# Decoder layer on one core: transposing q and k by DMA, and a new written-out order over more stages

## The chip, the core and the metric

The program runs on one core of a Trainium2 chip. The core has TensorE (matrix products, into PSUM), VectorE (DVE), ScalarE (ACT), GpSimd (POOL) and SyncE (SP, which here only issues DMAs). The engines run their own instruction streams and meet through semaphores. The metric is the device time of one execution in microseconds (us), lower is better.

## The reference

A pre-norm decoder layer on x of shape (32, 112, 256), batch by batch: attention, a cross block on ctx_1024 (32, 375, 256) that has a gelu in place of a softmax, and a quantised feed-forward block of 256, 1024, 256. Cut to its core:

```python
q = jnp.einsum('bim,mhd->bhid', x, wq)      # 8 heads of 128; k and v likewise
q = _rope(_rmsnorm(q)); k = _rope(_rmsnorm(k))
s = jnp.einsum('bhid,bhjd->bhij', q * mult, k * mult)   # minus 1e30 on later keys
p = jax.nn.softmax(s, axis=-1)
o = jnp.einsum('bhij,bhjd->bhid', p, v)
return jnp.einsum('bhid,hdm->bim', o, wo)
...
x = x + _L0_attn_ref(_layernorm(x, axis=-1), wq, wk, wv, wo)
x = x + _L0_xattn_ref(_layernorm(x, axis=-1), ctx_1024, ctx_1024)
x = x + _L0_ffn_ref(_layernorm(x, axis=-1), w1, b1, w2, b2)
```

## The kernel before, in words

The 32 batches are independent; one batch has 112 rows, which lie on 112 partitions. Every engine has one function `body(i)` that holds its work of round i for several batches at once: a = i is projected, b = i-1 goes through attention, c = i-2 through the cross block and the feed-forward's first layer, d = i-3 through its last. The order inside a body is written by hand for each engine; semaphores count finished steps. Rounds up to 3 and from 28 on are written out, those between run in a loop of four bodies (`iterations`).

Precision is had by splitting operands. A weight or activation is held as a rounded high half and the rest as a low half, and three products (high-high, high-low, low-high) are summed in PSUM. `project` (L846) forms q, k and v with 12 products of 512 columns each. q and k are squared on ScalarE (L697), summed on VectorE (L468), and the root is taken on GpSimd (L349, L351). The rotary step is a product with the cosines (L476), one with the sines (L485) and their sum (`turn`, L492), all on VectorE. `normalise_q` (L743, ScalarE, eight instructions) and `normalise_k` (L497, VectorE, one) scale by the root into `qkn` in fp32. TensorE transposes qkn by heads into PSUM (`transpose_qk`, L854, 16 matmul records a batch), ScalarE rounds the result to fp16 (`split_qkT`, L670) and VectorE forms the low half (L538). `scores` (L833, 24 products of 112 columns) follows, then exp, the causal mask on GpSimd (L362), `weigh_values` (L874), the division, `transpose_o` (L881), the split of oT (L545) and `project_out` (also L833, 24 products of 256 columns). The cross block is L911 (`ctx_hidden`) and L920 (`ctx_out`); the feed-forward is L937 (`hidden_units`) and L945 (`out_units`), with `x3b` = x3 + b2 on GpSimd (L355).

SyncE issues per round the store of a finished batch, `ctx_in` (L267) and `ctxT` (L270) of 375 KB each once the cross block has freed their buffers, and x (L264) of 112 KB.

## Time and profile before

| | us |
|---|---|
| median of 3 runs (lowest to highest) | 731.2 (730.33 to 732.17) |
| the profiled execution, device time | 730.79 |
| its span, first to last instruction | 729.1 |
| TensorE busy | 697.2 |
| VectorE busy | 642.4 |
| ScalarE busy | 486.9 |
| GpSimd busy | 248.3 |

The span is what the views of the trace divide. Busy time of an engine is the time in which it ran an instruction; an engine that is nearly always busy and carries the chain of work that ended last sets the time. Consecutive instructions of an engine overlap a little, so the distance from start to start is shorter than the duration. Matmul ends are modelled, so for TensorE too starts are the better measure.

### The profile page before, as it was taken

Reading aid. Unit: us, or ns where it says so; the run is one execution under the profiler, and the core shown is the slowest. Engines: PE = TensorE matmul, PEld = TensorE weight load, DVE = VectorE, ACT = ScalarE, POOL = GpSimd, SP = SyncE. Lnnn points to the kernel's source line nnn. Section 1 sums busy time; section 2 is a strip of 40 time slices with the busy share of each in tenths; the row PEclk is TensorE's granted clock in tenths of the full one; section 3 lists DMA queues with packets and bytes.
Section 4 is the critical chain, followed back from the end, with each engine's and each line's share of the span. In section 5 each row is a group of like instructions: output and inputs, shape, how many; then the busy total and the mean of one; then the engine's idle time right before and its main releaser. Section 6 shows DMA issues by size and latency. Waiting matters only on the chain.

```text
span 729.1 us, 15114 instructions
## 1 busy us (share of the span) xinstructions
PE 697.2 (96%) x5504; PEld 609.9 (84%) x5504; DVE 642.4 (88%) x1232; ACT 486.9 (67%) x1226; POOL 248.3 (34%) x393
## 2 busy tenths in 40 slices
PE   5599999999999999999999999999999999999974
PEld 4488888888888888888888989889888888888863
DVE  6989999999999999999999999999999999998942
ACT  5667766677766677776667767666777766677742
POOL 1344333433332343333234243333334333433310
PEclk9899999999999999999999999999999999999996
DMA  8501110111111011111111111101111110111100
GB/s 268 204 8 49 49 48 24 54 57 49 55 48 42 26 55 55 48 52 51 32 35 55 55 48 48 52 22 47 55 53 50 48 47 24 54 50 43 49 7 13
DMA packets 23946, 38.86 MB, mean 53 GB/s; under 512 B 2048, under 2 KB 18896, under 8 KB 23664
## 3 DMA queue, kind: packets, MB, share of 16 engines
q1 hardware_dynamic: 23920, 38.51, 17.5%
q8 instruction: 16, 0.26, 0.2%
q14 instruction: 10, 0.08, 0.0%
HBM read 34.84 MB, written 3.67 MB: 53 GB/s over the span
## 4 chain that ended last, share of the span: by engine, by line
PE 89%; DVE 3%; ACT 3%; issue 2%; DMA 2%; SPq 0%; POOL 0%; POOLq 0%; DVEq 0%; ACTq 0%
PE psum L846 34%; PE psum L833 17%; PE psum L874 7%; PE psum L854 6%; PE psum L911 6%; PE psum L920 6%; PE psum L945 4%; PE psum L937 3%; PE psum L881 3%; PE psum L902 2%; DMA w_raw<-in_wv 1%; DMA w_raw<-in_w 1%; ACT qkn L743 1%; PE psum L927 1%; DVE turn_c L492 0%
## 5 line engine op out<-in xcount | busy, mean ns | idle before, releaser
L846 PE MATMUL psum<-wqkv_hi,xnT_hi 128*112 128x512 f32 x384 | 165.1, 430 | 4.8 <-DVE wqkv_lo L433 2.8
L846 PE MATMUL psum<-wqkv_lo,xnT_hi 128*112 128x512 f32 x384 | 152.3, 397 | 0.0
L846 PE MATMUL psum<-wqkv_hi,xnT_lo 128*112 128x512 f32 x384 | 131.4, 396 | 0.0
L697 ACT ACTIVATE sq<-psum 112x1024 f32<-112x1024 f32 x64 | 65.5, 1023 | 79.7 <-PE psum L846 79.7
L344 POOL TENSOR_TENSOR rstd<-ve,nhalf 112x1 f32<-112x1 f32 x96 | 55.4, 578 | 156.0 <-DVE ve L407 151.0
L351 POOL TENSOR_TENSOR rms<-ms,nhalf 112x8 f32<-112x8 f32 x64 | 106.3, 1662 | 5.0
L733 ACT ACTIVATE w_raw<-psum,rden 112x128 f32<-112x128 f32 x256 | 69.5, 384 | 45.7 <-DVE rden L519 45.7
L846 PEld LDWEIGHTS psum<-wqkv_hi,xnT_lo 128*112 128x112 f32 x384 | 67.5, 176 | 22.1
L846 PEld LDWEIGHTS psum<-wqkv_hi,xnT_hi 128*112 128x112 f32 x384 | 68.1, 177 | 21.4 <-issue 3.1
L476 DVE TENSOR_TENSOR turn_c<-psum,cos_t 112x1024 f32<-112x1024 f32 x64 | 78.1, 1220 | 6.2 <-ACT sq L697 5.6
L468 DVE TENSOR_REDUCE ss<-sq 112x4 f32<-112x512 f32 (+1 forms) x95 | 81.9, 862 | 0.0
L846 PEld LDWEIGHTS psum<-wqkv_lo,xnT_hi 128*112 128x112 f32 x384 | 68.4, 178 | 16.1
L743 ACT ACTIVATE qkn<-turn_c,rms 112x128 f32<-112x128 f32 x256 | 81.4, 400 | 0.1
L833 PE MATMUL psum<-wo_hi,oT_hi 128*112 128x256 f32 x256 | 78.3, 306 | 0.8 <-DVE oT_lo L545 0.8
L492 DVE TENSOR_TENSOR turn_c<-turn_c,turn_s 112x1024 f32<-112x1024 f32 x64 | 77.9, 1217 | 0.1
L485 DVE TENSOR_TENSOR turn_s<-psum,sin_t 112x1024 f32<-112x1024 f32 x64 | 77.5, 1210 | 0.0
L833 PE MATMUL psum<-wo_hi,oT_lo 128*112 128x256 f32 x256 | 71.6, 280 | 0.0
L833 PE MATMUL psum<-wo_lo,oT_hi 128*112 128x256 f32 x256 | 71.6, 280 | 0.0
L538 DVE TENSOR_TENSOR qkT_lo<-psum,qkT_hi 128x896 f16<-128x896 f32 x64 | 69.4, 1085 | 0.2
L757 ACT ACTIVATE f_int<-psum,b_col 128x112 int16<-128x112 f32 x256 | 65.8, 375 | 1.8 <-PE psum L937 1.8
L874 PEld LDWEIGHTS psum<-v_sb,w_raw 112*112 112x112 f32 x512 | 60.8, 176 | 3.6
L874 PE MATMUL psum<-v_sb,w_raw 112*112 112x129 f32 x512 | 62.0, 273 | 0.0
(82 smaller groups left out, 1531.4 us busy)
## 6 DMA issues: line engine op xcount, KB each, us to landing
ctx_in<-in_ctx_rows SPq DMA_DIRECT2D x32, 375.0 KB
ctxT<-in_ctx_cols SPq DMA_DIRECT2D x32, 375.0 KB, 6.4
x_in<-in_x SPq DMA_DIRECT2D x32, 112.0 KB, 2.0
out_y<-y_out SPq DMA_DIRECT2D x32, 112.0 KB, 1.9
w_raw<-in_w SPq DMA_DIRECT2D x2, 1024.0 KB, 7.5
w_raw<-in_wq SPq DMA_DIRECT2D x2, 512.0 KB, 4.6
w_raw<-in_wk SPq DMA_DIRECT2D x2, 512.0 KB, 6.3
w_raw<-in_wv SPq DMA_DIRECT2D x2, 512.0 KB, 8.0
```

Source lines behind the costliest of these rows:

```text
L351: pool.tensor_tensor(rms[:, w, :], ms[:, w, :], nhalf[:, 0:H], ALU.pow).then_inc(qk_rms_done[w], 1)
L468: return dve.tensor_reduce(ss[:, w, hs], heads(sq[:, w, :])[:, hs, :], AX_X, ALU.add)
L476: dve.tensor_tensor(turn_c[:, w, :].rearrange("t (b h d) -> t b h d", b=2, d=D), (q_ps, k_ps)[w].rearrange("t b (h d) -> t b h d", d=D), c ...
L485: dve.tensor_tensor(turn_s[:, w, :].rearrange("t (h two f) -> t h two f", two=2, f=HALF), halves, table, ALU.mult).then_inc(sin_done[w], 1)
L492: dve.tensor_tensor(turn_c[:, w, :], turn_c[:, w, :], turn_s[:, w, :], ALU.add).then_inc(qk_turned[w], 1)
L538: dve.tensor_tensor(qkT_lo[:, w, :].rearrange("p (b n) -> p b n", b=2), (qT_ps, kT_ps)[w], qkT_hi[:, w, :].rearrange("p (b n) -> p b n", b=2),
L733: last = act.activation(on[:, h * D:(h + 1) * D], o_ps[:, h // OH, (h % OH) * VW:(h % OH) * VW + D], ACT.Copy, scale=rden[:, h:h + 1])
L743: last = act.activation(qkn[:, 0, h * D:(h + 1) * D], turn_c[:, 0, h * D:(h + 1) * D], ACT.Copy, scale=rms[:, 0, h:h + 1])
L757: last = act.activation(f_int[:, c * T:(c + 1) * T], f_ps[:, c // (FC // 2), (c % (FC // 2)) * T:(c % (FC // 2) + 1) * T], ACT.Relu, bias= ...
L833: product = pe.matmul(dst, lh, rh, start=first and k == 0, stop=last and k == len(terms) - 1)
L846: last = pe.matmul(ps[:, n, :], left[:, c, :], right[:, c, w, n * BANK:(n + 1) * BANK], start=c == 0 and left is xnT_hi and right is wqkv_ ...
L874: last = pe.matmul(o_ps[:, h // OH, at:at + VW], p_sb[:, h * T:(h + 1) * T], v_sb[:, h, :], start=h % OH == 0, stop=h % OH == OH - 1 or h ...
```

## The change

- The transposes of q and k leave TensorE. ScalarE scales and rounds each head to fp16 (`round_q0`, `round_q1`, `round_k0`, `round_k1`, eight instructions for each of q and k) into `qk16`, VectorE forms the low half there with one scalar_tensor_tensor a head (`split_q`, `split_k`, eight each), and SyncE issues two transposing DMAs a batch, each of 112 x 2048 fp16 (high and low halves side by side) into `qkT` of 128 x 16 x 112. `scores` waits for their landing.
- `normalise_k` on VectorE and `split_qkT` on ScalarE and VectorE are gone.
- The sum of the keys' rotary products moves to GpSimd (`turn_k`); that of the queries stays on VectorE (`turn_q`).
- The loop is gone: the bodies for i = -3 to 35 are all written out. A batch is loaded in round j-3, its q and k are projected in j-2, v in j-1, scores in j, the output projection in j+1, the cross block in j+1 and j+2, the feed-forward in j+3 and j+4. PSUM banks are laid out anew for this, and many waits that the order implies are left out.
- On SyncE a round is: store, ctx_in, x, ctxT, then the two transposes.

The diff, cut to its core ("..." marks what is left out):

```diff
-        qkn = sb("qkn", [T, 2, HD])
-        qkT_hi = sb("qkT_hi", [P, 2, H * T], F16)
-        qkT_lo = sb("qkT_lo", [P, 2, H * T], F16)
+        qk16 = sb("qk16", [T, 2, 2, HD], F16)
+        qkT = sb("qkT", [P, 2, 2 * H, T], F16)
...
+        v0_ps, v1_ps = psum[0:T, 6, :], psum[0:T, 0, :]
+        s_ps = psum[0:T, 3:5, 0:HH * T]
...
-        def iterations(eng, body):
-
-            end = B - UNROLL
-            for i in (FIRST, SECOND, THIRD):
-                body(i)
-            for n in range(2, UNROLL):
-                body(Batch(0, n))
-            with eng.Fori(1, end // UNROLL) as turn:
-                base = eng.snap(turn * UNROLL)
-                for u in range(UNROLL):
-                    body(Batch(base, u))
-            for n in range(end, B + 3):
-                body(Batch(0, n))
...
+            def transpose_k(j):
+                sp.wait_ge(k_lo_done, done(j))
+                sp.dma_start_transpose(qkT[:, 1], qk16[:, 1].rearrange("t l n -> t (l n)")).then_inc(kT_landed, 16)
+
+            def transpose_q(j):
+                sp.wait_ge(q_lo_done, done(j))
+                sp.dma_start_transpose(qkT[:, 0], qk16[:, 0].rearrange("t l n -> t (l n)")).then_inc(qT_landed, 16)
...
+                a, c, d, h = (Batch(i + 3), Batch(i + 1), Batch(i - 0), Batch(i - 4))
+                if h.inside(B):
+                    store_out(h)
+                if d.inside(B):
+                    load_ctx(d)
+                if a.inside(B):
+                    load_x(a)
+                if d.inside(B):
+                    load_ctxT(d)
+                if c.inside(B):
+                    if c.off == 0:
+                        load_weights()
+                    transpose_k(c)
+                    transpose_q(c)
+
+            for i in range(-3, B + 4):
+                body(i)
             for s in range(SLOTS):
...
+            def turn_k(j):
+                pool.wait_ge(k_sin_done, done(j))
+                pool.tensor_tensor(turn_c[:, 1, :], turn_c[:, 1, :], turn_s[:, 1, :], ALU.add).then_inc(k_turned, 1)
...
+                b, c, d, e, f, g = (Batch(i + 2), Batch(i + 1), Batch(i - 0), Batch(i - 1), Batch(i - 2), Batch(i - 3))
+                if c.inside(B):
+                    rms_root_k(c)
+                if d.inside(B):
+                    mask_later_keys(d)
+                if b.inside(B):
+                    variance_x(b)
+                if e.inside(B):
+                    root_x2(e)
+                if b.inside(B):
+                    root_x(b)
+                if c.inside(B):
+                    rms_root_q(c)
+                if g.inside(B):
+                    add_b2(g)
+                if b.inside(B):
+                    turn_k(b)
+                if f.inside(B):
+                    root_x3(f)
...
+            def split_k(j):
+                if j.off == B - 1:
+                    dve.wait_ge(k_hi0_done, done(j))
+                for h in range(H):
+                    at = slice(h * D, (h + 1) * D)
+                    last = dve.scalar_tensor_tensor(out=qk16[:, 1, 1, at], in0=turn_c[:, 1, at], scalar=rms[:, 1, h:h + 1],
+                                                    in1=qk16[:, 1, 0, at], op0=ALU.mult, op1=ALU.subtract)
...
+                a, b, c, d, e, f, g, h = (Batch(i + 3), Batch(i + 2), Batch(i + 1), Batch(i - 0), Batch(i - 1), Batch(i - 2), Batch(i - 3), Batch(i - 4))
+                if c.inside(B):
+                    turn_q(c)
+                if h.inside(B):
+                    residual_out(h)
+                if e.inside(B):
+                    normalise_x2(e)
+                if b.inside(B):
+                    split_xnT(b)
+                    if b.off == 0:
+                        split_projections()
+                if c.inside(B):
+                    split_k(c)
+                if f.inside(B):
+                    residual_ctx(f)
+                if c.inside(B):
+                    split_q(c)
+                    if c.off == 0:
+                        clip_weights(0)
+                        clip_weights(1)
+                        fixed_biases()
+                        split_wo(0)
+                        split_wo(1)
+                if d.inside(B):
+                    split_oT0(d)
+                if b.inside(B):
+                    turn_cos_k(b)
+                    turn_sin_k(b)
+                if f.inside(B):
+                    stats_x3(f)
+                if b.inside(B):
+                    sum_squares_k(b)
+                    turn_cos_q(b)
+                if d.inside(B):
+                    split_oT1(d)
+                if g.inside(B):
+                    clip_hidden1(g)
+                if f.inside(B):
+                    quantise_x3(f)
+                if g.inside(B):
+                    clip_hidden0(g)
+                if b.inside(B):
+                    turn_sin_q(b)
+                if f.inside(B):
+                    clip_x3(f)
+                if e.inside(B):
+                    gelu_inner(e)
+                if a.inside(B):
+                    stats_x(a)
+                if d.inside(B):
+                    residual_attention(d)
+                    stats_x2(d)
+                if e.inside(B):
+                    gelu_outer(e)
+                if b.inside(B):
+                    sum_squares_q(b)
+                if c.inside(B):
+                    invert_sums(c)
+                if a.inside(B):
+                    normalise_x(a)
...
+            def round_k1(j):
+                act.wait_ge(k_rms_done, done(j))
+                for h in range(1 * HH, 2 * HH):
+                    last = act.activation(qk16[:, 1, 0, h * D:(h + 1) * D], turn_c[:, 1, h * D:(h + 1) * D],
+                                          ACT.Copy, scale=rms[:, 1, h:h + 1])
+                last.then_inc(k_hi1_done, 1)
...
+            def scores(j):
+                pe.wait_ge(qT_landed, landed_once(j))
+                pe.wait_ge(kT_landed, landed_once(j))
+                if j.has(4):
+                    pe.wait_ge(f0_int_done, done(j.plus(-4)))
+                if j.off == 0:
+                    pe.wait_ge(k_sin_done, done(j.plus(1)))
...
+                    dst = s_ps[:, h // HH, (h % HH) * T:(h % HH + 1) * T]
+                    q_hi, q_lo, k_hi, k_lo = qkT[:, 0, h, :], qkT[:, 0, H + h, :], qkT[:, 1, h, :], qkT[:, 1, H + h, :]
+                    pe.matmul(dst, k_hi, q_hi, start=True, stop=False)
+                    pe.matmul(dst, k_hi, q_lo, start=False, stop=False)
+                    last = pe.matmul(dst, k_lo, q_hi, start=False, stop=True)
...
+                b, c, d, e, f, g, h = (Batch(i + 2), Batch(i + 1), Batch(i - 0), Batch(i - 1), Batch(i - 2), Batch(i - 3), Batch(i - 4))
+                if e.inside(B):
+                    transpose_o1(e)
+                    project_out0(e)
+                    project_out1(e)
+                if d.inside(B):
+                    scores(d)
+                if e.inside(B):
+                    project_out3(e)
+                    project_out2(e)
+                if c.inside(B):
+                    project_v0(c)
+                if d.inside(B):
+                    weigh_values(d)
+                if g.inside(B):
+                    transpose_xq(g)
+                if h.inside(B):
+                    out_units(h)
+                if c.inside(B):
+                    project_v1(c)
+                if b.inside(B):
+                    transpose_xn(b)
+                if f.inside(B):
+                    ctx_out(f)
+                if d.inside(B):
+                    transpose_o0(d)
+                if e.inside(B):
+                    transpose_xn2(e)
+                if b.inside(B):
+                    project_k(b)
+                if g.inside(B):
+                    hidden_units1(g)
+                if b.inside(B):
+                    project_q(b)
+                if g.inside(B):
+                    hidden_units0(g)
+                if e.inside(B):
+                    ctx_hidden(e)
```

## Rows read from the trace of the kernel before

**Rows 1.** the profile page: engines' busy time, and shares of the chain that ended last
```profile
PE 697.2 (96%) x5504; PEld 609.9 (84%) x5504; DVE 642.4 (88%) x1232; ACT 486.9 (67%) x1226; POOL 248.3 (34%) x393
...
PE 89%; DVE 3%; ACT 3%; issue 2%; DMA 2%; SPq 0%; POOL 0%; POOLq 0%; DVEq 0%; ACTq 0%
```

**Rows 2.** windows over the whole run: us, busy us of each engine, clock, DMA share, GB/s
```profile
0.00:48.00 48.00, 31.55 (x167) 24.51 (x168) 38.91 (x57) 30.32 (x50) 13.68 (x25) 0.93 0.52 180
48.00:689.20 641.20, 641.14 (x5153) 566.07 (x5151) 588.00 (x1133) 442.41 (x1135) 229.32 (x358) 1.00 0.16 47
689.20:729.10 39.90, 24.47 (x190) 19.32 (x187) 15.46 (x44) 14.12 (x42) 5.34 (x10) 0.83 0.03 9
```

**Rows 3.** windows, one steady round
```profile
312.00:333.39 21.39, 21.39 (x175) 18.90 (x174) 19.62 (x39) 14.79 (x39) 7.65 (x12) 1.00 0.16 47
```

**Rows 4.** timeline of TensorE, a steady round: start us, us, engine, line, operation
```profile
325.69 1.70 PE L854 MATMUL psum<-ident,qkn 112*128 112x112 f32 x16
327.16 0.46 PE L846 MATMUL psum<-wqkv_hi,xnT_hi 128*112 128x512 f32 x1
327.46 0.40 PE L846 MATMUL psum<-wqkv_lo,xnT_hi 128*112 128x512 f32 x1
```

**Rows 5.** chain of work in a steady round: start us, us, piece
```profile
52.91 1.25 PE psum L833 x24
...
58.40 1.77 PE psum L874 x16
60.17 1.30 PE psum L920 x6
...
67.58 1.46 PE psum L833 x12
69.04 1.60 PE psum L854 x16
70.64 2.80 PE psum L846 x12
73.44 0.87 PE psum L945 x8
```

**Rows 6.** groups by line: busy us, mean ns, idle before
```profile
L743 ACT ACTIVATE qkn<-turn_c,rms 112x128 f32<-112x128 f32 x256 | 81.4, 400 | 0.1
...
L492 DVE TENSOR_TENSOR turn_c<-turn_c,turn_s 112x1024 f32<-112x1024 f32 x64 | 77.9, 1217 | 0.1
...
L538 DVE TENSOR_TENSOR qkT_lo<-psum,qkT_hi 128x896 f16<-128x896 f32 x64 | 69.4, 1085 | 0.2
```

**Rows 7.** timeline of VectorE in a steady round
```profile
327.04 0.41 DVE L398 BATCH_NORM_STATS2 stat<-x_in 112x6 f32<-112x256 f32 x1
327.38 0.18 DVE L403 BATCH_NORM_AGGREGATE mv<-stat 112x2 f32<-112x6 f32 x1
```

**Rows 8.** groups by line, GpSimd
```profile
L355 POOL TENSOR_TENSOR x3b<-x,b_rows 112x256 f32<-112x256 f32 x32 | 23.5, 735 | 0.0
...
L349 POOL TENSOR_TENSOR ms<-ss,rms_eps 112x8 f32<-112x8 f32 x64 | 14.1, 220 | 77.6 <-DVE ss L468 77.6
```

**Rows 9.** timelines of VectorE and of GpSimd near 688 us
```profile
688.26 1.68 DVE L497 TENSOR_TENSOR qkn<-turn_c,rms 112x1024 f32<-112x1024 f32 x1
...
688.13 0.73 POOL L355 TENSOR_TENSOR x3b<-x,b_rows 112x256 f32<-112x256 f32 x1
```

**Rows 10.** line L497: its instructions, duration ns min/median/max
```profile
L497 DVE TENSOR_TENSOR qkn<-turn_c,rms x32: 1215/1540/1691, 26.6 to 688.3; 112x1024 f32<-112x1024 f32 x32
```

**Rows 11.** the page's DMA issues: KB each, median us to landing
```profile
ctxT<-in_ctx_cols SPq DMA_DIRECT2D x32, 375.0 KB, 6.4
```

**Rows 12.** windows during the weight load and during a steady context load
```profile
22.00:23.00 1.00, 1.00 (x5) 0.76 (x4) 1.00 (x2) 1.00 (x1) 1.00 (x1) 0.66 1.02 371
...
323.00:324.00 1.00, 1.00 (x18) 0.95 (x17) 1.00 (x2) 1.00 (x4) 1.00 (x1) 1.00 0.31 119
```

**Rows 13.** timeline of SyncE's queue in a steady round
```profile
318.82 0.39 SPq L270 DMA_DIRECT2D ctxT<-in_ctx_cols  x1
```

More of the change, by code:

```diff
@@ new lines, in store_out, with load_ctx @@
+            def store_out(j):
+                sp.wait_ge(out_done, done(j))
+                sp.dma_start(out[j.at].rearrange("o t m -> (o t) m"), y_out[:, j.off % SLOTS, :]).then_inc(out_stored[j.off % SLOTS], 16)
+            def load_ctx(j):
+                if j.has(2):
+                    sp.wait_ge(ctxout_ready, done(j.plus(-2)))
+                sp.dma_start(ctx_in[:, j.off % 2], ctx_rows[j.at].rearrange("o (p c) m -> (o p) c m", c=SC)).then_inc(
+                    ctx_landed[j.off % SLOTS], 16)
@@ L390, in _ @@
+            for i in range(-3, B + 4):
+                body(i)
         @block.vector
@@ L667, in _ @@
+            for i in range(-3, B + 4):
+                body(i)
         @block.scalar
@@ new lines, in project_out @@
+            def project_out(heads, j, first, last):
+                if is_first(j):
+                    pe.wait_ge(wo_done, 3)
+                for h in heads:
+                    pe.matmul(y_ps, oT_hi[:, h, :], wo_hi[:, h, :], start=first and h == heads[0], stop=False)
+                    pe.matmul(y_ps, oT_hi[:, h, :], wo_lo[:, h, :], start=False, stop=False)
+                    product = pe.matmul(y_ps, oT_lo[:, h, :], wo_hi[:, h, :], start=False, stop=last and h == heads[-1])
+                return product
@@ new lines, in out_units, with project_v1, transpose_xn @@
+            def out_units(j):
+                if j.off == B - 1:
+                    pe.wait_ge(f0_q_done, done(j))
+                for c in range(FC):
+                    last = pe.matmul(f2_ps, f_q[:, c, :], w2T[:, c, :], start=c == 0, stop=c == FC - 1)
+                last.then_inc(f2_ready, 1)
+            def project_v1(j):
+                if j.has(3):
+                    pe.wait_ge(g_done, done(j.plus(-3)))
+                project(2, 1, v1_ps, j).then_inc(v1_ready, 1)
+            def transpose_xn(j):
+                pe.wait_ge(xn_done, done(j))
+                transpose_rows(xnT_ps, xn1).then_inc(xnT_ready, 1)
@@ new lines, in ctx_out, with transpose_o0 @@
+            def ctx_out(j):
+                pe.wait_ge(ctx_landed[j.off % SLOTS], landed(j))
+                if j.has(1):
+                    pe.wait_ge(xqT_copied, done(j.plus(-1)))
+                if j.off >= B - 3:
+                    pe.wait_ge(g_done, done(j))
+                for c in range(SC):
+                    last = pe.matmul(ctx_ps, g[:, c * T:(c + 1) * T], ctx_in[:, j.off % 2, c, :], start=c == 0, stop=c == SC - 1)
+                last.then_inc(ctxout_ready, 1)
+            def transpose_o0(j):
+                pe.wait_ge(o0_normed, done(j))
+                if j.has(4):
+                    pe.wait_ge(out_done, done(j.plus(-4)))
+                for h in range(0 * HH, 1 * HH):
+                    last = pe.transpose(oT_ps0[:, (h % HH) * T:(h % HH + 1) * T], on[:, h * D:(h + 1) * D], ident[0:T, 0:T])
+                last.then_inc(oT0_ready, 1)
@@ new lines, in project_q, with hidden_units0 @@
+            def project_q(j):
+                if j.has(4):
+                    pe.wait_ge(x3_done, done(j.plus(-4)))
+                if 3 <= j.off <= 4:
+                    pe.wait_ge(xn2T_copied, done(j.plus(-3)))
+                project(0, 0, q_ps[:, 0, :], j)
+                project(0, 1, q_ps[:, 1, :], j).then_inc(q_ready, 1)
+            def hidden_units0(j):
+                if is_first(j):
+                    pe.wait_ge(w_q_done, 2)
+                for c in range(0 * FC // 2, 1 * FC // 2):
+                    for m in range(MC):
+                        last = pe.matmul(f0_ps[:, (c % (FC // 2)) * T:(c % (FC // 2) + 1) * T], w1T[:, m, c, :], xqT[:, m, :],
+                                         start=m == 0, stop=m == MC - 1)
+                last.then_inc(f0_ready, 1)
@@ L913, in ctx_hidden @@
                 last.then_inc(h_ready, 1)
-            def ctx_out(j):
-                pe.wait_ge(g_done, done(j))
-                pe.wait_ge(ctx_landed[j.off % SLOTS], landed(j))
-                for c in range(SC):
-                    last = pe.matmul(ctx_ps, g[:, c * T:(c + 1) * T], ctx_in[:, j.off % 2, c, :],
-                                     start=c == 0, stop=c == SC - 1)
-                last.then_inc(ctxout_ready, 1)
-            def transpose_xq(j):
-                pe.wait_ge(xq_done, done(j))
-                for m in range(MC):
-                    last = pe.transpose(xqT_ps[:, m * T:(m + 1) * T], xq[:, m * P:(m + 1) * P], ident_b[0:T, 0:T])
-                last.then_inc(xqT_ready, 1)
@@ L1023, in tables_of @@
+            for i in range(-3, B + 4):
+                body(i)
 def tables_of(T, D):
```

989 lines of the change are left out of this document (405 added, 584 removed).

## The prediction

> **What bounds the kernel now.** I read the busy shares and the chain of work first. TensorE is busy for 697.2 of 729.1 us and carries 89% of the chain [rows 1]. The split into three stretches says where the rest lies [rows 2]: in the 641.2 us of the steady stretch TensorE stands still for 0.1 us; in the first 48 us it idles 16.5 us, in the last 39.9 us it idles 15.4 us. In one steady round of 21.39 us TensorE is busy all through, VectorE 19.62, ScalarE 14.79, GpSimd 7.65 us, at the full granted clock of 2.4 GHz [rows 3]. So a batch costs what its TensorE instructions cost, and VectorE follows 1.8 us behind. 32 x 21.39 is 684.5 us; the other 44.6 us are the 31.9 us of idle time at both ends and 12.7 us of work stretched there by a granted clock of 0.93 and 0.83.
>
> **The round on TensorE.** Only the 16 matmul records that transpose qkn leave. In a steady round they start at 325.69 and the next group at 327.16, so they take 1.47 us [rows 4]; the chain of another round gives them 1.60 [rows 5]. The new round is 21.39 - 1.5 = 19.9 us. Project, scores, weigh, context and MLP keep their counts; a change of group costs its first matmul under 0.1 us more, and the new order has one or two more such changes, so I take 19.95. Gain: 1.44 x 32 = 46 us, the main term.
>
> Writing the loop out costs nothing: the steady stretch of before holds looped rounds and written-out ones (its last four), and TensorE idles in neither [rows 2].
>
> **What the DVE does instead.** It loses two splits of the transposed halves (L538, 1.085 each), the key normalisation (L497, median 1.54) and one rotary sum (L492, 1.22) [rows 6, 10]; consecutive operations overlap by some 0.1 us, so these free about 4.6 us. It gains 16 scalar_tensor_tensor of 112x128. No row has this form. The nearest: bn_stats of 256 elements is followed 0.34 us later by the next instruction [rows 7], and 1024 elements take 1.217 - 0.09 = 1.13; the slope is 1.03 ns an element with 0.08 us fixed, so 0.21 us for 128, and 16 of them 3.3 us. Bounds: 0.17 (128 ns and nothing else much) to 0.34 (a 256-element step), 2.7 to 5.4 us; I take 3.3, since both rows lie on one line. DVE: 19.6 - 4.6 + 3.3 = 18.3 us, under TensorE's 19.95 by 1.6.
>
> **Keys' sum on GpSimd.** x3b (112x256) takes 735 ns and an 8-wide addition 220 [rows 8]: 2.08 ns an element and 2.3 us for 1024 elements; four whole x3b, 2.9 us, is the upper end. GpSimd comes to 10 to 10.6 us of 19.95. Behind turn_k on its queue only root_x3 stands, for which the DVE waits at quantise_x3. Between turn_sin_k and quantise_x3 the DVE has two operations of 1.13 us and stats, split and clip, about 3.7 us, against 2.3 + 0.55 = 2.9 (3.5 at the upper end), so it is just hidden. ScalarE loses the two qkT_hi copies (about 1.8 us) and gains eight key roundings like L743, 0.40 us and overlapping [rows 6] (about 2.3), thus stays near 15.3 us: nothing.
> GpSimd's wide addition also slows the DVE: the key normalisation that started at 688.26 beside x3b (688.13, 0.73 us) took 1.68 us, the fastest of its line 1.215 [rows 9, 10]: 0.45 us lost in 0.6 us of overlap. With turn_k this is 0 (the DVE's operations beside it read PSUM or one tile) to 0.75 x 2.3 = 1.7 us a round; I take 0.6, which the 1.6 us of slack hide. At the upper end the DVE is level with TensorE and its in-order waits show: 0.3 to 0.8 us a round, 10 to 25 us in all.
> The Trainium skill (VectorE: DVE Perf Modes, "Two Vector instructions with no wait between them") says the second SBUF read interface of a DVE instruction with two SBUF inputs is shared with GpSimd. By that rule the sums and PSUM readers beside turn_k lose nothing, and the sum would be without the 0.6; the trace agrees for the normalisation that was slowed, and has no wide GpSimd addition beside a reduction.
>
> **The transposing DMAs, the term that decides.** Two per batch, each 112 x 2048 fp16 = 448 KB, on the same queue as the 862 KB of loads and 112 KB store. While SP waits for k_lo or q_lo, only the next round's store and loads stand behind it; while scores wait, all of TensorE does. No row shows a transposing transfer. Where they must fit, by adding up the pieces of [rows 5] in the new order, zero at transpose_o1: scores start at 0.4 + 1.4 = 1.8 us, ctx_out ends at 11.5 (scores 1.25, four heads' output projection 1.46, v0 half of 2.80, weigh 1.77, 0.1, out_units 0.87, v1 1.40, 0.2, ctx_out 1.30). SP's order puts the store, load_ctx, load_x and load_ctxT ahead of both transposes, and load_ctx waits for ctx_out, so the loads are issued from 11.5 on. split_xnT follows transpose_xn at about 10.8, hence split_k runs from 11.1 to 12.7, split_q to 14.8. The transposes are issued at about 12.8 and 14.8, and the next scores stand at 19.9 + 1.8 = 21.7. That is 6.9 us for the second.
> Loads take their share first. ctxT lands 6.4 us after its issue [rows 11], because ctx_in in front of it occupies only 0.31 of the 16 engines, that is five, at 119 GB/s or 24 KB/us each [rows 12]. Those five are held by ctx for 384/119 = 3.2 us, by ctxT and x for about 1.3 more: free at about 17.2. Of ctxT's 6.4 us these engines' work is 3.2 + 1.0, so start and completion take 2.2, of which I put 1.2 at the end. If a transposing transfer moves like a plain one (371 GB/s in the weight load [rows 12], 23 KB/us an engine), each of the 16 engines needs 57 KB/24 = 2.4 us for both, and with the completion both have landed at 20.8, 0.9 us before they are needed. A lower end than this there is not; at 16 KB/us the pair lands 1.3 us later and stalls 0.4 us a round, at 12 KB/us 1.6 us, at 8 KB/us 4.0. The stall repeats every round: ctx_out, load, transposes, scores, ctx_out is a closed chain, 9.7 us of TensorE work plus what the DMAs take. I take 0 to 0.4, since the nearest rows are plain transfers at 23 to 24 KB/us an engine.
> The Trainium skill (Advanced Engine Details and Errata, "X-Bar Transpose (TRN2)") says transposing transfers are as fast as regular ones; DMA: Bandwidth & Descriptors ("Latency and other measured facts") gives 261 GB/s for one kernel. By the latter an estimate is 3.5 us for both, landing 0.2 to 0.4 us late, and a sum some 12 us higher.
>
> **Fill and drain.** A batch now passes from round j-2 (projections) to j+4 (out_units), where before it was transposed and scored one round after its projection. In the fill, normalise_x of the next batch stands last in the DVE's round, behind all rotary work of the first, and scores(0) wait for k_sin(1) and behind the weight conversions. Adding up the durations in the orders, I get about 34 us of TensorE idle before steady state against 16.5, and 12 to 15 at the end against 15.4: +15 us, an estimate, 5 to 25. Slow-clock work 10 to 13 as before.
>
> **Sum.** Span 729.1 - 46 + 15 - 1 = 697; the profiled execution took 1.7 us more than its span (730.8), and the median of the runs is 0.4 over that: 699. With the DMAs free of stall and no further group changes it would be 692; with 0.4 us a round of stall 711.
>
> **Rivals.**
> (a) Transposing transfers slow or late: slower than before. For: nothing in the trace shows their rate; the queue is shared, the five low engines are behind ctx; only 0.9 us of slack. Against: DMA engines are busy for 16% of a round. Point: the saved 46 less the 15 of fill is 1.0 us a round, so from 1.9 us behind my landing time on, the kernel is slower. At a third of the plain rate (8 KB/us an engine, 7.2 us a pair) the round is 19.9 + 4.0 = 23.9 and the time 699 + 128 = 827; at half (12) the round is 21.5 and the time 750. Chance 0.27, mostly 735 to 830.
> (b) SP issues one transpose for microseconds instead of the 0.39 of a load [rows 13]. With x each, landing is 12.8 + 2x + 2; it decides from x = 3.4 us on, and at 4 us costs 2.4 us a round: 775. Chance 0.06. 
> (c) DVE or GpSimd become the bound (contention at its upper end, or 0.3 us for a split): round 20.3 to 20.9, 710 to 730. Chance 0.17.
> (d) The transposes off TensorE bring nothing, because the stage's real limit is elsewhere: within 0.3% of before, 0.04. Against it: TensorE has no idle time in the steady stretch.
>
> **How the numbers follow.** Forecast (round 19.85 to 20.4, 690 to 712): 0.46. (a) 0.27, (b) 0.06, (c) 0.17, (d) 0.04. Faster by over 0.3% (about what these runs can tell from no change): 0.46 + 0.17 = 0.63; same 0.04; slower 0.33. The likeliest case gives 699, its own range is 690 to 712. The wide range goes from 688 up to 800, which leaves out the upper part of (a) and little below.
>
> **What would show it.** The spacing of the first project matmuls in the middle: 19.9 us if right. The wait of scores for a DMA: none or under 0.4 us; if it is there in every round, (a) or (b), told apart by issue time on SP and time to landing (I expect the pair landed 6 us after the second issue). turn_k at 2.3 to 2.9 us, key splits at 0.21 us apart, the reduction beside turn_k at 1.2 us (more: contention). TensorE idle of about 34 us before 110 us. The prediction fails if the transposes land over 8.8 us after the second's issue.

## The result and the profile after

The changed kernel takes 747.6 us (median of four runs, 745.3 to 748.8) against 731.2 us: a ratio of 1.022 with a 95% interval of 1.0192 to 1.0248. It is slower by 16 us, a difference well clear of the scatter, where a gain to 699 us was forecast. 699 us is what the same kernel reaches when one order of issue on SP is changed (experiment 1 below). That 699.3 is the median of four runs, one of which (704.5) was in a slower state; the other three have a median of 697.8.

The page of the kernel after: busy time and count of each engine, then the shares of the chain that ended last, then its DMA issues (number, median us to landing). They answer to [rows 1, 11].

```profile
PE 665.5 (90%) x4992; PEld 566.1 (76%) x4992; DVE 622.8 (84%) x1585; ACT 502.4 (68%) x1418; POOL 317.9 (43%) x425
...
PE 41%; SPq 20%; DMA 19%; DVE 11%; ACT 5%; issue 2%; POOL 1%; ACTq 0%; DVEq 0%; POOLq 0%
SPq L259 19%; DMA qkT<-qk 19%; DVE qk L452 8%; PE psum L896 8%; PE psum L829 4%; PE psum L831 4%; PE psum L830 4%; PE psum L910 3%; PE psum L839 3%; PE psum L875 3%; PE psum L841 2%; PE psum L840 2%; PE psum L877 2%; PE psum L876 2%; ACT xn
...
ctxT<-in_ctx_cols SPq DMA_DIRECT2D x32, 375.0 KB, 6.8
```

TensorE lost its 512 matmuls, but its share of the chain fell from 89% to 41%. L259 is `transpose_k`'s issue on SP: 19% of the chain is SP issuing, another 19% the transfers in flight. The three stretches (us, busy us of PE, PEld, DVE, ACT, POOL, then granted clock, DMA share, GB/s), as in [rows 2]:

```profile
0.00:112.50 112.50, 83.89 (x504) 67.44 (x505) 89.89 (x195) 69.85 (x165) 42.76 (x62) 0.92 0.43 120
112.50:675.00 562.50, 530.93 (x4059) 453.67 (x4058) 494.46 (x1280) 398.20 (x1147) 257.99 (x338) 0.98 0.48 90
675.00:743.30 68.30, 50.69 (x431) 44.97 (x429) 38.42 (x114) 34.33 (x108) 17.13 (x25) 0.89 0.38 69
```

In the middle TensorE now idles for 31.6 us, where it idled for 0.1. TensorE's waits in that stretch (us in total, times, longest) are one line, and that line is a wait in nearly every round:

```profile
PE psum L875 <- DMA qkT<-qk: 31.6, 26, 2.3
```

L875 is the first matmul of `scores` (line numbers shift by a few from kernel to kernel below). One round, from SP's queue (start us, us of issue):

```profile
324.06 0.26 SPq L243 DMA_DIRECT2D ctx_in<-in_ctx_rows  x1
324.37 0.32 SPq L251 DMA_DIRECT2D x_in<-in_x  x1
324.73 0.42 SPq L254 DMA_DIRECT2D ctxT<-in_ctx_cols  x1
325.67 5.06 SPq L259 DMA_TRANSPOSE qkT<-qk  x1
330.78 2.21 SPq L263 DMA_TRANSPOSE qkT<-qk  x1
```

and from the chain of waits in the same round (start us, us, piece):

```profile
322.77 0.37 ACT xnT_hi L645
323.20 0.26 issue
323.46 2.19 DVE qk L452 x8
325.67 5.06 SPq L259
330.78 5.34 DMA qkT<-qk
336.16 0.26 PE psum L875
```

The keys are split into their halves at 325.67 and SP takes 5.06 us to issue their transpose. The queries' transpose cannot be issued before 330.78, though DVE finished its split at 328.07. It lands at 336.12, and by then TensorE has waited 1.95 us for it at `scores`. Over all rounds (duration ns min/median/max, and us to landing):

```profile
L259 SPq DMA_TRANSPOSE qkT<-qk x32: 1379/4914/5366, 28.9 to 695.3; - x32
...
DMA to landing us min/median/max: 3.5/7.6/9.5
```

The minimum, 1.38 us and 3.5 us to landing, belongs to the first three rounds, in which the last load ahead had been issued over 7 us before. So the question was what makes an issue of 1.4 us one of 5. One thing can be read from this trace already. In the middle the first transpose starts 1.6 us behind the issue of `ctx_in` in most rounds and 2.3 to 2.5 in three; its issue takes 4.3 to 5.4 us in the former and 3.9 to 4.1 in the latter. It ends 6.0 to 7.0 us behind the issue of `ctx_in` in both.

### The profile page after: what moved, and what is told of

Same layout as the page of the kernel before. It is cut to its first block, busy times and chain, and to the rows that moved or that the text cites. A ratio compares the mean times of both kernels' runs of the same rounds, so it can differ in the third digit from the quotient of the medians.

```text
span 743.3 us, 13995 instructions
## 1 busy us (share of the span) xinstructions
PE 665.5 (90%) x4992; PEld 566.1 (76%) x4992; DVE 622.8 (84%) x1585; ACT 502.4 (68%) x1418; POOL 317.9 (43%) x425
## 2 busy tenths in 40 slices
DMA packets 140724, 68.76 MB, mean 93 GB/s; under 512 B 118784, under 2 KB 135632, under 8 KB 140400
## 4 chain that ended last, share of the span: by engine, by line
PE 41%; SPq 20%; DMA 19%; DVE 11%; ACT 5%; issue 2%; POOL 1%; ACTq 0%; DVEq 0%; POOLq 0%
SPq L259 19%; DMA qkT<-qk 19%; DVE qk L452 8%; PE psum L896 8%; PE psum L829 4%; PE psum L831 4%; PE psum L830 4%; PE psum L910 3%; PE psum L839 3%; PE psum L875 3%; PE psum L841 2%; PE psum L840 2%; PE psum L877 2%; PE psum L876 2%; ACT xnT_hi L645 1%
## 5 line engine op out<-in xcount | busy, mean ns | idle before, releaser
L340 POOL TENSOR_TENSOR turn_c<-turn_c,turn_s 112x1024 f32<-112x1024 f32 x32 | 76.3, 2383 | 271.3 <-DVE turn_s L389 271.3
L829 PE MATMUL psum<-wqkv_hi,xnT_hi 128*112 128x512 f32 x384 | 161.4, 420 | 7.8 <-DVE wqkv_lo L395 5.0
L831 PE MATMUL psum<-wqkv_hi,xnT_lo 128*112 128x512 f32 x384 | 153.3, 399 | 0.0
L712 ACT ACTIVATE w_raw<-psum 112x896 f32<-112x896 f32 x32 | 29.4, 919 | 111.3 <-PE psum L877 111.3
L875 PE MATMUL psum<-qkT 128*112 128x112 f16 x256 | 46.1, 229 | 49.5 <-DMA qkT<-qk 40.5
L830 PEld LDWEIGHTS psum<-wqkv_lo,xnT_hi 128*112 128x112 f32 x384 | 68.9, 179 | 15.4
L875 PEld LDWEIGHTS psum<-qkT 128*112 128x112 f16 x256 | 35.7, 139 | 56.3 <-DMA qkT<-qk 46.9
L840 PE MATMUL psum<-wo_lo,oT_hi 128*112 128x256 f32 x256 | 74.8, 292 | 0.0
L841 PE MATMUL psum<-wo_hi,oT_lo 128*112 128x256 f32 x256 | 74.7, 292 | 0.0
L452 DVE SCALAR_TENSOR_TENSOR qk<-turn_c,rms,qk 112x128 f16<-112x128 f32 x256 | 70.3, 348 | 0.0
L466 DVE SCALAR_TENSOR_TENSOR qk<-turn_c,rms,qk 112x128 f16<-112x128 f32 x256 | 69.9, 346 | 0.0
L545 DVE TENSOR_TENSOR x<-psum,x_in 112x256 f32<-112x256 f32 x32 | 13.6, 424 | 46.0 <-PE psum L841 45.9
```

The costliest lines, as they stand in the source:

```text
L452: last = dve.scalar_tensor_tensor(out=qk16[:, 1, 1, at], in0=turn_c[:, 1, at], scalar=rms[:, 1, h:h + 1], in1=qk16[:, 1, 0, at], op0=ALU.m ...
L829: pe.matmul(dst, xnT_hi[:, c, :], wqkv_hi[:, c, w, cols], start=c == 0, stop=False)
L830: pe.matmul(dst, xnT_hi[:, c, :], wqkv_lo[:, c, w, cols], start=False, stop=False)
L831: last = pe.matmul(dst, xnT_lo[:, c, :], wqkv_hi[:, c, w, cols], start=False, stop=c == MC - 1)
L840: pe.matmul(y_ps, oT_hi[:, h, :], wo_lo[:, h, :], start=False, stop=False)
L841: product = pe.matmul(y_ps, oT_lo[:, h, :], wo_hi[:, h, :], start=False, stop=last and h == heads[-1])
```

## Experiments

**Theory A:** the transposes are held up by the loads that SP issues just ahead of them. It has two forms: A1, by the five DMA engines that `ctx_in` occupies [rows 12]; A2, by the loads' bytes in all. **Rival B:** the transposes are slow by themselves. **Rival C:** VectorE or GpSimd is the bound and the DMA wait only shows it.

**1. The transposes ahead of the loads in SP's body.**

```diff
                 if h.inside(B):
                     store_out(h)
-                if d.inside(B):
-                    load_ctx(d)
-                if a.inside(B):
-                    load_x(a)
-                if d.inside(B):
-                    load_ctxT(d)
                 ...
                     transpose_k(c)
                     transpose_q(c)
+                if a.inside(B):
+                    load_x(a)
+                if d.inside(B):
+                    load_ctxT(d)
+                    load_ctx(d)
```

> SyncE's round is: store, k transpose, q transpose, x, ctxT, ctx (the loads behind the transposes), nothing else changed. Theory A (the transposes queue behind the context loads: SyncE needs 5.1 us to issue the first because the loads ahead fill the queues, and TensorE waits for the second's landing): both issues fall to about 1.5 us as in the first rounds, the pair lands 3.6 us after the second issue, scores no longer wait, round 19.9 us, time about 702 us. Rival B (a transposing DMA costs this much by itself in steady state, beside five busy engines, whatever lies ahead of it): issue stays near 5 and 2.2 us, round 21.6, time 745 to 750.

Measured: 699.3 us, ratio 0.959 (0.9544 to 0.9634). SP's queue in a round, and the windows:

```profile
331.73 1.47 SPq L259 DMA_TRANSPOSE qkT<-qk  x1
334.17 1.47 SPq L263 DMA_TRANSPOSE qkT<-qk  x1
335.68 0.58 SPq L251 DMA_DIRECT2D x_in<-in_x  x1
336.30 0.43 SPq L254 DMA_DIRECT2D ctxT<-in_ctx_cols  x1
336.78 0.37 SPq L243 DMA_DIRECT2D ctx_in<-in_ctx_rows  x1
```

```profile
0.00:112.50 112.50, 84.02 (x508) 67.74 (x508) 90.43 (x196) 70.64 (x165) 43.91 (x62) 0.94 0.40 119
112.50:620.00 507.50, 506.42 (x3982) 436.39 (x3982) 482.01 (x1247) 388.26 (x1115) 254.79 (x329) 1.00 0.40 99
620.00:691.40 71.40, 58.02 (x506) 51.01 (x504) 48.77 (x144) 44.22 (x139) 22.76 (x35) 0.99 0.28 71
```

Each issue is 1.47 us, each landing 3.5 to 3.6 us after its issue starts, TensorE idles 1.1 us in the middle 507, and the mean spacing of the keys' issues there is 19.93 us. Theory A holds. B falls: a transpose alone is fast enough. C falls too for the kernel after, since VectorE and GpSimd do the same work here in 50 us less. The pair has landed at 337.8 and the next scores start at 340.10: 2.3 us of slack.

**2. ctx_in's load spread over more engines**, the order left as it was: 112 partitions and 13 as two DMAs.

```diff
-                sp.dma_start(ctx_in[:, j.off % 2], ctx_rows[j.at].rearrange("o (p c) m -> (o p) c m", c=SC)).then_inc(
-                    ctx_landed[j.off % SLOTS], 16)
+                rows = ctx_rows[j.at].rearrange("o (p c) m -> (o p) c m", c=SC)
+                sp.dma_start(ctx_in[0:112, j.off % 2], rows[0:112]).then_inc(ctx_landed[j.off % SLOTS], 16)
+                sp.dma_start(ctx_in[112:SP, j.off % 2], rows[112:SP]).then_inc(ctx_landed[j.off % SLOTS], 16)
```

> The ctx_in load of 125 partitions is cut in two, 112 partitions and 13, so that its bytes go to all 16 DMA engines; order unchanged. Theory A1 (the 3.2 us in which ctx_in holds five engines is what blocks the first transpose's issue): issue of the first falls from 5.1 to about 2.5 us, landing 2.5 us earlier, stall of scores gone, time about 703 us. Rival A2 (the block is the 862 KB of loads as such, or their number of descriptors): issue of the first stays over 4 us, time 738 to 748.

Measured: 707.0 us (0.9653 to 0.9707). The issue of the keys' transpose fell from a median of 4.9 us to 3.55 (2.2 to 4.5 in steady rounds), its landing from 7.6 to 6.2; the issue lies between what A1 (2.5) and A2 (over 4) expected. TensorE waited for the pair for 10.2 us in all, against 40.5 in the kernel after. So 1.4 us less of issue, under half of what the loads add to it, was worth 41 of the 48 us, because TensorE's wait was only 1.2 us a round. The five engines are a part of the hold, not all of it.

**3. Both edits.**

> Both edits together. Theory A: nothing is left to gain after the first edit, round 19.9 us, about 702 us, within 3 us of the first edit alone. If something else than the loads stalls scores, it is still there: over 715 us.

Measured: 694.65 us (0.9482 to 0.9535), issue 1.48 us, mean round 19.99. It is the fastest kernel here. Its lead over the first (699.3, single runs 693.4 to 704.5) is within that one's scatter, and its round is no shorter.

**4. The keys' rotary sum back on VectorE**, all else as changed.

```diff
 # VectorE's body                # GpSimd's body
                 if b.inside(B):
+                    turn_k(b)
                     sum_squares_k(b)
-                    turn_k(b)   # there
```

> The keys' rotary sum goes back from GpSimd to VectorE, ahead of its sum of squares; all else as in the changed kernel. While the transposes set the round, VectorE's extra 1.13 us (its busy time goes to about 19.4 us of 21.6) shifts the splits of k and q by up to that: 747 to 770 us. Rival (the sum on GpSimd slows VectorE and is part of the loss): faster than 745 us.

Measured: 749.2 us (1.022 to 1.0285). VectorE gained 44 us of work and the time stayed within the scatter: while TensorE waits for the DMA, where this sum runs is of next to no account. The slack is small, though: TensorE's wait for the pair fell from 40.5 us in all to 32.7, and VectorE carries 45% of the chain instead of 11%.

**5 and 6. Which load holds them.** In 5, ctx_in alone goes behind the transposes, and SP still waits for `ctx_out` ahead of x, so that x and ctxT are issued no earlier than before; in 6, ctx_in alone stays ahead.

```diff
 # 5                            # 6
+ wait for ctxout_ready
+ load_x, load_ctxT             + load_ctx
+ transpose_k, transpose_q      + transpose_k, transpose_q
+ load_ctx                      + load_x, load_ctxT
```

> The order of the changed kernel with one move: ctx_in's load (375 KB on five DMA engines) goes behind the two transposes; x and ctxT stay ahead of them. If ctx_in's five engines are what holds the transposes (theory A1), SP issues the k transpose in 1.5 to 2.3 us instead of 5, TensorE's wait for the pair falls from 1.4 us a round to 0 to 0.2, and the time is 697 to 706. If it is every load ahead, by its bytes (theory A2: 487 of 862 KB still stand ahead), the issue stays at 2.5 to 4 us and the time is 707 to 725.

> The counterpart: ctx_in's load alone stays ahead of the transposes, x and ctxT go behind them. Theory A1 (five engines held for 3.2 us): k transpose still issued in 3.5 to 5 us, time 725 to 745. Theory A2 (by bytes, 375 of 862 KB): issue 2.5 to 3 us, time 700 to 712.

Measured: 704.0 us (0.9581 to 0.9639) and 700.6 us (0.955 to 0.959). In 6:

```profile
130.00 0.27 SPq L243 DMA_DIRECT2D ctx_in<-in_ctx_rows  x1
132.85 1.48 SPq L259 DMA_TRANSPOSE qkT<-qk  x1
...
332.85 0.27 SPq L243 DMA_DIRECT2D ctx_in<-in_ctx_rows  x1
334.46 2.54 SPq L259 DMA_TRANSPOSE qkT<-qk  x1
337.05 2.67 SPq L263 DMA_TRANSPOSE qkT<-qk  x1
```

With ctx_in alone ahead the time and the issues of the later rounds (1.7 to 3.0 us) are as A2 had them, and the wait is gone (1.3 us in all of the middle); A1 forecast 725 to 745 and misses. The two rounds shown differ in the distance of the load. In the first six rounds of the middle ctx_in is issued 2.85 us before the keys' transpose, and that takes 1.4 to 1.5 us; in the later ones it is 1.6 us, and 1.7 to 3.0. So it matters how long before the transpose a load was issued; here 1.2 us more are enough to be rid of the hold. In 5, with x and ctxT alone ahead, the issue is 1.49 us, as A1 had it; but there 2.1 us passed between the end of ctxT's issue and the keys' split, against 0.5 in the kernel after, so these 487 KB had time to drain and the run does not refute A2. Neither half of the loads holds the transposes long enough to matter; the two together do. Whether bytes or ctx_in's engines count for more stays open.

Experiment 5 has no DMA wait and still is not faster than 1. VectorE carries 70% of its chain and is busy for 643.6 us with the very instructions that took 621.2 in 1: here rival C is real. Its timeline, then GpSimd's:

```profile
331.07 1.22 DVE L428 TENSOR_TENSOR turn_c<-turn_c,turn_s 112x1024 f32<-112x1024 f32 x1
...
333.65 2.66 DVE L454 SCALAR_TENSOR_TENSOR qk<-turn_c,rms,qk 112x128 f16<-112x128 f32 x8
...
346.82 0.76 DVE L376 TENSOR_SCALAR xq<-xq_int 112x256 bf16<-112x256 int16 x1
```

```profile
331.06 2.74 POOL L333 TENSOR_TENSOR rms<-ms,nhalf 112x8 f32<-112x8 f32 x1
333.77 0.82 POOL L338 TENSOR_TENSOR x3b<-x,b_rows 112x256 f32<-112x256 f32 x1
...
346.52 0.98 POOL L312 TENSOR_SCALAR_AFFINE_SELECT w_raw<-w_raw 112x896 f32<-112x896 f32 x1
```

The root of the queries (1.65 us in experiment 1, where it starts 0.37 us before `turn_q`) takes 2.74 when it starts together with it: 1.09 longer, about the length of `turn_q` (1.22). It pushes x3b onto the key splits: the eight of them take 2.66 us beside x3b where they take 2.19 alone, and the clip of xq (0.217 us in experiment 1) takes 0.76 and ends just behind the mask's 0.98. The order of issue on SP changed which operations of the two engines coincide, and the round is 0.5 us longer (20.4 against 19.9). That the one causes the other is read from these timelines; no run takes it apart.

**7. The loads on ScalarE's queue**, right behind `round_xnT`; SP keeps the store and the transposes.

> The three loads are issued by ScalarE on its own queue, right behind round_xnT, so at about the same time of the round as before; SP's queue holds the store and the two transposes alone. If the transposes wait because SP's own queue is in order and full behind the loads (queue theory), the issue is back at 1.4 to 1.6 us, the landing 3.6 to 4.5 us after it, the time 700 to 712. If they wait because the DMA engines themselves are busy with the loads (engine theory), the issue stays at 3.5 to 5 us, the wait of scores over 1 us a round and the time at 735 to 755. ScalarE's three issues of 0.4 us cost it 1.2 us of some 4 us of slack: nothing by either.

Measured: 748.9 us (1.0229 to 1.0273), and for neither reason given. Chain of waits, one round, then TensorE's waits from 112 to 600 us (in total, times, longest):

```profile
328.24 1.31 PE psum L930 x6
329.57 0.27 ACTq L746
...
330.84 1.28 ACT qk L733 x4
332.12 1.18 ACT qk L739 x4
333.32 1.18 DVE qk L443 x5
334.64 0.89 DVE qk L443 x3
335.54 5.94 DMA qkT<-qk
341.52 0.26 PE psum L876
```

```profile
PE psum L961 <- ACT v_sb L622: 29.3, 23, 2.1
PE psum L876 <- DMA qkT<-qk: 5.3, 7, 1.2
```

L746 is `load_ctx`, which waits for `ctx_out` (L930). On ScalarE the query roundings (L733, L739) stand behind that wait, and everything behind them is late. In the round shown that is the split, the transpose and the scores. In most rounds it is ScalarE's copy of v, for which `hidden_units1` (L961) waits: 29.3 us against 5.3 for the DMA. It is the same kind of loop, through another engine. "Nothing by either" for ScalarE was wrong, because I counted the issues' durations and not the wait in front of them. What the run does show: with the loads on another queue the issues take 2.2 and 2.6 us (medians) against 4.9 and 2.2. In some rounds the keys' transpose follows the loads at the same 1.6 us as in the kernel after, and even there it takes 2.4 to 2.9 us against 4.3 to 5.4. The first still lands 6.7 us after its issue against 7.6. So about half of the 5 us is the shared queue, and most of the delay to landing is not.

**8. The keys transposed four times** (three times into tiles that nothing reads; scores wait for all), on experiment 1.

```diff
                 sp.dma_start_transpose(qkT[:, 1], qk16[:, 1]...)
+                for n in range(3):
+                    sp.dma_start_transpose(spare[:, n], qk16[:, 1]...)
```

> The kernel with both transposes ahead of the loads, and k transposed four times (three copies into tiles that nothing reads; scores wait for all). With both transposes first, q's is issued at 334.17 and lands 3.6 us later in a round whose next scores start at 340.15, so there are 2.4 us of slack. If transposes pass one after the other at 1.47 us of SP's issue each, q's issue moves by 4.4 - 1.0 us (it waits 1.0 us for q_lo now), to 3.4 us later, its landing is 1.0 us late, the round 19.9 + 1.0 = 20.9 and the time 725 to 740. If the DMA engines and not the issue set the pace (over 2 us a transpose), the round grows by 2.5 us or more and the time is over 770. If the engines run them side by side and only the issue counts, but the chain isn't closed over the round, no change: 699.

Measured: 855.8 us (1.1665 to 1.1726). Windows of the middle and of one us behind a wait of TensorE, then SP's queue, then the first matmuls of scores in this kernel:

```profile
130.00:730.00 600.00, 523.25 (x3720) 452.28 (x3718) 453.66 (x1165) 363.43 (x1047) 237.87 (x312) 0.91 0.58 133
...
342.00:343.00 1.00, 1.00 (x6) 1.00 (x6) 0.00 (x0) 1.00 (x4) 0.96 (x2) 0.50 0.24 98
```

```profile
327.21 1.47 SPq L260 DMA_TRANSPOSE qkT<-qk  x1
328.72 5.58 SPq L262 DMA_TRANSPOSE spare<-qk  x3
334.34 1.73 SPq L266 DMA_TRANSPOSE qkT<-qk  x1
```

```profile
L877 PE MATMUL psum<-qkT 128*112 128x112 f16 x256 | 68.4, 291 | 115.0 <-DMA qkT<-qk 106.0
```

From the keys' issue to the queries' landing (334.34 + 4.0) it is 11.1 us against 6.0 in experiment 1: 5.1 more, of which 2.3 is slack, so 2.8 a round should show. TensorE's idle time grew by (855.3 - 711.8) - (691.4 - 648.5) = 100.6 us, 3.1 a round: the loop over the round is closed. The expectation's first case had put one transpose behind another at 1.47 us each and got 1.0 us a round; the three copies take 1.86 each (5.58 in all), and the time is that of its second case, over 770. TensorE's busy time grew too, by 711.8 - 648.5 = 63 us, at a granted clock of 0.91: the scores' matmuls right after the wait take 291 ns against 217. Behind the wait the granted clock is 0.50 for some microseconds, so 1.2 GHz instead of 2.4. I had left this term out, here and in the prediction.

**9. Each transpose in two halves**, on experiment 1.

> The kernel with the transposes ahead of the loads, each transpose cut into its two 112 x 1024 halves, so four issues a batch. If SP's 1.47 us of issue go by the elements transposed, each half takes 0.7 to 0.8 us and the second half lands 3.6 us after the first's issue as now: time 697 to 702. If they are a price for each DMA, each half takes 1.4 us, q's second half is issued 1.5 to 2 us later than now and 2.4 us of slack just hold it: 699 to 712, with waits of scores for the DMA in some rounds.

Measured: 697.5 us (0.9527 to 0.958). Line of the keys' halves:

```profile
L260 SPq DMA_TRANSPOSE qkT<-qk x64: 1222/1294/2252, 28.8 to 651.3; - x64
...
DMA to landing us min/median/max: 2.6/2.7/4.3
```

Half the elements take 1.29 us of issue instead of 1.47: nearly all of it is a price for each DMA. The time is that of the other case (697 to 702), for the slack held all four issues. Landing falls from 3.55 to 2.7 us, so by an estimate 224 KB take 0.85 us: 270 GB/s, or 17 KB/us an engine. Experiment 8's three copies, 1.38 MB issued in 5.58 us, give 247 GB/s.

**10 and 11. The keys' sum back on VectorE where no DMA wait covers it**: on experiment 5 and on experiment 1.

> The kernel with only ctx_in behind the transposes (704 us, VectorE on 70% of its chain, its clip of xq at 773 ns where it takes 217 elsewhere, key splits at 402 ns where they take 348) with the keys' sum back on VectorE. If GpSimd's sum beside the clip is what slows VectorE there (contention theory), the clip is back at 217 to 230 ns; VectorE gains 0.56 us and loses 1.2 us a round, and the time is 703 to 715. If the clip stays over 500 ns, the sum on GpSimd is not its cause.

> The kernel with the transposes ahead of the loads and the keys' sum back on VectorE: what its place on GpSimd is worth once the DMA wait is gone. VectorE is busy for 90% of 691 us there, 18.5 us of a round of 19.9; with 1.2 us more it is at 19.7, level with TensorE. If VectorE's in-order waits show when it is level, the round is 20.2 to 20.7 and the time 708 to 725; if 0.2 us of slack suffice, 699 to 703.

Measured: 724.6 (0.9897 to 0.9931) and 724.7 us (0.989 to 0.9931). So the move of this one sum is worth 25 us on experiment 1 and 21 on experiment 5, against 2, within the scatter, while the transposes are late (experiment 4). VectorE carries 75% of the chain in both; in 11 the middle reads

```profile
112.50:640.00 527.50, 506.55 (x3921) 433.40 (x3919) 512.42 (x1262) 392.75 (x1113) 246.72 (x302) 1.00 0.37 92
```

with TensorE idle for 21 us of 527 at full clock. In 10 the clip of xq is back at 216 ns, by which its expectation would blame the sum on GpSimd. The timeline of 5 suggests otherwise: the clip stands beside the mask, and the sum, further up GpSimd's queue, may only have delayed the mask into it. No run tells the two apart. 724.6 lies above the 703 to 715 of the expectation, although its terms were right: 1.2 us of the sum less 0.56 of the clip is 0.6 us a round, and the round grew by that, from 20.38 to 20.93. VectorE had no slack to hide any of it.

## Why the prediction was wrong, point by point

**The step that failed is the issue of the transposing DMAs on SP.** I take `transpose_o1` as zero again: it starts at 310.81 in the round shown, and the 1.34 us that this round's own scores waited are taken off. The keys' transpose was issued at 13.5 us, forecast 12.8; the queries' at 18.6, forecast 14.8; the pair landed at 24.0, forecast 20.8; scores could have begun at 22.1, forecast 21.7. Of the 3.8 us by which the queries' issue was late, 2.7 are SP, still busy with the keys' issue after the split had ended at 328.07; the rest is the later start and the dearer splits. I took the issue to be 0.39 us as for a load [rows 13], and let SP's next issue depend on nothing but `q_lo`. That row was of a plain load; a transpose is 1.47 us with no load under way, and 5 us behind 862 KB of loads. I had counted the loads' hold on the engines (to 17.2), but only against the transfer, never against the issue. Rival (b) named the right place, "SP issues one transpose for microseconds", with a chance of 0.06 and a cause that is not the one found (a price of the transpose alone: that is 1.47 us, not the 3 of its estimate). The measured pair, 5.06 + 2.21, is 3.6 us each, just over its turning point of 3.4. Its sum was wrong besides: by its own formula 4 us each land at 22.8, 1.1 us late and not 2.4, so some 734 us and not 775; and 3.6 each would land at 22.0, where 24.0 was measured, since the loads hold the transfer too. Rival (a), late behind the loads, was right in its mechanism and its sign; its sizes (735 to 827) came from a slow rate. The two cases belong together: the issue is long because the loads are ahead. That 747.6 is near the 750 of its half rate is luck, for the rate was not halved. The pair deserved more than 0.33 in sum, since experiment 1 shows how much rested on an order the diff printed plainly: 862 KB issued 1.6 us ahead of the thing that TensorE waits for.

**The sign of failure was measured from the wrong point.** I had written that the prediction fails if the pair lands over 8.8 us after the second issue. The point where gain turns to loss was 1.9 us behind a landing 6.0 us after that issue, so 7.9. It landed 5.3 us after it, sooner than forecast, and the kernel was slower all the same: the issue itself was late, and the sign could not see that.

**The rate.** Forecast 24 KB/us an engine with the plain loads, measured 17 (the estimate of experiment 9). By the Trainium skill (Advanced Engine Details and Errata, "X-Bar Transpose (TRN2)") transposing transfers are as fast as regular ones; experiment 9's 270 GB/s beside the 371 of [rows 12] does not bear that out. The Trainium skill's page DMA: Bandwidth & Descriptors ("Latency and other measured facts") gives 261 GB/s for one kernel with a non-contiguous middle dimension. That is near the 270, but the source here is contiguous, so whether it is the same effect is not shown. At 17 KB/us the pair would have landed 1.0 us later than I had it, by itself 0.1 us late: this term alone would not have decided.

**What the wait costs: a term left out.** After against experiment 1, the spans differ by 743.3 - 691.4 = 51.9 us. TensorE's idle time makes (743.3 - 665.5) - (691.4 - 648.5) = 34.9 of it, its longer busy time 665.5 - 648.5 = 17.0. The latter is the clock's: the mean granted clock is 0.967 against 0.989. It did not fall behind every wait. Of the 26 in the middle it fell behind five, of 1.88, 1.91, 1.93, 1.97 and 2.28 us; it stayed at 1.00 behind two as long (1.95, in the round shown, and 2.01) and behind all of 1.81 and less. Two microseconds behind the longest of them:

```profile
422.00:424.00 2.00, 2.00 (x16) 2.00 (x15) 0.00 (x0) 1.19 (x3) 0.20 (x2) 0.50 0.00 0
```

Each of the five costs about 1.7 us of work at the lower clock; most of the rest of the 17 us lies at the end, behind waits of 2.2 and 5.2 us (clock 0.89 from 675 us on, against 0.99 in experiment 1's last stretch). The break-even (a stall of 1.0 us a round) took only idle time. Idle time alone would have given 699.3 + 34.9 = 734 us; the clock made the rest.

**The round on TensorE: right, once the wait is gone.** 19.93 us in experiment 1, forecast 19.95, with 1.1 us of idle time in the whole middle; with the wait the kernel after has 21.66.

**Fill and drain: right.** Idle outside the middle is 28.6 + 17.6 us after (7.4 of the latter are two waits for the transposes) and 28.5 + 13.4 in experiment 1, forecast about 34 + 12 to 15, and 16.5 + 15.4 before.

**VectorE's splits: mis-sized.** Eight take 2.19 us, 0.27 each where I took 0.21 (bounds 0.17 to 0.34): 1.0 us a round more. The two rows through which I laid the line were of other operations.

**The sum on GpSimd: right in size** (2.38 us, forecast 2.3 to 2.9), and neither the reduction (1.21 us) nor the PSUM readers (1.22) beside it were slowed, so the 0.6 was too much there. The move was worth more than I had it: by experiment 11 VectorE could not have carried the sum in a round of 19.9. The contention that exists is elsewhere on the two engines and shows in experiment 5 (x3b beside the key splits, 0.47 us a round; the root beside `turn_q`, 1.09). Rival (c) came true there with a round of 20.4, inside its 20.3 to 20.9, though the 704.0 us lie under its 710 to 730. The Trainium skill (VectorE: DVE Perf Modes, "Two Vector instructions with no wait between them") names the read interface that a two-input VectorE instruction shares with GpSimd; the root that ran 1.09 us longer beside `turn_q` agrees.

With the order of experiment 1 the forecast of 699 is met within the scatter of its runs (693.4 to 704.5); that its median lies 0.3 us off is chance. The fill was some 5 us cheaper than I had it, and the dearer splits stayed under TensorE.

## What to carry to other kernels

When a transfer moves onto the path between two engines, ask what its own queue has issued in the last few microseconds: its issue can be blocked as well as its transfer, and everything behind it in the queue is late with it. Put what the busiest engine waits for ahead of prefetches that have a whole round of time. Price a long wait of TensorE above its length, since the clock may fall behind it. And a step whose move brings nothing beside a longer wait may be worth 25 us once that wait is gone, so take parts out and put them back again after the bound has moved.

## What the runs showed of the hardware that I had not expected

- SP issues a transposing DMA of 112 x 2048 fp16 in 1.47 us and one of half the size in 1.29; with 862 KB of loads issued from 1.6 us ahead it takes 4.9 (median), with 375 KB issued 1.6 us ahead 1.7 to 3.0 and 2.85 us ahead 1.4 to 1.5, with the 862 KB on another queue 2.2.
- The 64 transposes added 140,724 - 23,946 = 116,778 DMA packets (the pages' counts after and before), about 1,825 each, and 116,736 of these are under 512 B.
- TensorE waits of 0.3 to 2.3 us, one in nearly every round, took the mean clock of the middle from 1.00 to 0.98, by falls behind five of them; waits of some 3 us a round took it to 0.91.
- GpSimd's root of 8 values a partition took 2.74 us instead of 1.65 when a two-input addition on VectorE started with it, and 1.65 when it had started 0.37 us before.
